# The hand-over from the recurrence to the expert layer: last logits laid out by a product, last row sums on VectorE, the end of the router moved into the first phase

## The reference, cut to what matters

```
xn = x * rsqrt(mean(x*x) + 1e-6) * norm_w ; x_branch, gate = split(xn @ W_in.T)
xc = silu(conv4(x_branch)) ; dt = clamp(softplus(xc @ W_dt.T + b)) ; B, C = xc @ W_B.T, xc @ W_C.T
h[t] = h[t-1] * exp(clamp(dt*A)) + dt*B*xc ; every 10th step h *= min(20/|h|, 1)
y = sum over n of h*C + D*xc            (16 states n per channel)
x2 = layernorm(x + (x + scale * (y*silu(gate)) @ W_out.T))
p = softmax(x2 @ w_router) ; the two largest of 8 experts per token, gates p/(p1+p2)
place of a token in its expert = running count over the 8192 tokens, kept if below 768
out = layernorm(x2 + sum of gate * expert(x2))      (expert: 256 -> 1024 -> relu -> 256)
```

## Time and profile before

| what | us |
|---|---|
| median of three executions | 2680.76 |
| the profiled execution, its own time | 2680.78 |
| its span in the trace | 2678.6 |
| last operation of the first phase (VectorE, LGS) | 2277.6 |
| first operation of the second phase | 2281.1 |
| first product of the counts | 2288.4 |

### The profile page before, as it was taken

The page is one execution under the profiler, slowest core; times in us unless marked ns, Lnnn a source line. Parts: engine busy times, 40 slices in busy tenths (PEclk is TensorE's granted clock), DMA queues, the critical chain, the costliest instruction groups (busy, mean ns, idle before and its releaser), DMA issues. The chain is left out here.

```text
span 2678.6 us, 50407 instructions
## 1 busy us (share of the span) xinstructions
PE 2564.4 (96%) x16600; PEld 2364.2 (88%) x16600; DVE 2376.2 (89%) x3459; ACT 2207.0 (82%) x4934; POOL 2189.3 (82%) x2270
## 2 busy tenths in 40 slices
PE   7999999999999999999999999999999988899997
PEld 6899999999999999999999999999999987677775
DVE  6999999999999999999999999999999998412245
ACT  5999999999999999999999999999999994211122
POOL 4898888889888888989888888989888896654546
PEclk9999999999999999999999999999999999699999
DMA  3222222222222222222222222222222222443464
GB/s 98 63 75 80 78 82 76 80 76 80 75 80 79 77 80 79 77 80 75 79 79 81 77 78 77 75 80 78 80 76 83 70 78 58 136 100 69 109 209 145
DMA packets 147569, 228.26 MB, mean 85 GB/s; under 512 B 39660, under 2 KB 85612, under 8 KB 146156
## 3 DMA queue, kind: packets, MB, share of 16 engines
q1 hardware_dynamic: 124228, 189.22, 24.2%
q0 software_dynamic: 11040, 15.15, 3.0%
q10 hardware_dynamic: 12040, 20.67, 2.3%
HBM read 190.85 MB, written 34.10 MB: 84 GB/s over the span
## 5 line engine op out<-in xcount | busy, mean ns | idle before, releaser
L1065 POOL TENSOR_TENSOR H<-H,CB 128x640 f32<-128x640 f32 (+1 forms) x824 | 1206.0, 1478 | 122.8 <-DVE H L808 120.9
L808 DVE TENSOR_TENSOR_SCAN H<-DA,PM 128x704 f32<-128x704 f32 (+1 forms) x824 | 1297.4, 1595 | 0.0
L521 ACT ACTIVATE DA<-DT,SM 128x160 f32<-128x160 f32 (+1 forms) x3200 | 1068.9, 422 | 1.5 <-POOL DT L956 0.3
L1101 PE MATMUL YB<-H,ID 128*128 128x160 f32 (+1 forms) x6592 | 1032.5, 308 | 0.2 <-POOL H L1065 0.2
L1101 PEld LDWEIGHTS YB<-H,ID 128*128 128x128 f32 x6592 | 971.2, 190 | 16.4 <-issue 11.2
L776 DVE TENSOR_TENSOR PM<-PM,BB 128x640 f32<-128x640 f32 (+1 forms) x824 | 667.4, 810 | 0.2
L530 ACT ACTIVATE DA<-DA 128x2560 f32<-128x2560 f32 x204 | 473.1, 2320 | 1.7
L973 POOL TENSOR_TENSOR FC<-SN,HALF 128x4 f32<-128x4 f32 x206 | 232.4, 1128 | 38.7 <-DVE SN L815 34.7
L1114 PE MATMUL PAZ<-XN,RB 128*128 128x160 f32 x1648 | 249.6, 305 | 7.8 <-POOL XN L940 4.4
L1124 PEld LDWEIGHTS PAZ<-XB,CD 128*128 128x128 f32 x1664 | 237.5, 188 | 16.8
L1124 PE MATMUL PAZ<-XB,CD 128*128 128x160 f32 x1664 | 243.1, 297 | 0.0
(11 more groups left out here) (205 smaller groups left out, 2968.0 us busy)
## 6 DMA issues: line engine op xcount, KB each, us to landing
BB<-Bd SPq DMA_DIRECT2D x208, 320.0 KB, 3.4
CB<-Cd SPq DMA_DIRECT2D x206, 320.0 KB, 3.4
W<-in_w ACTq DMA_DIRECT2D x16, 1024.0 KB, 8.1
XT<-in_xT SPq DMA_DIRECT2D x52, 160.0 KB, 2.2
XR<-in_xp SPq DMA_DIRECT2D x208, 40.0 KB
X2d<-VV SPq DMA_DIRECT2D x208, 40.0 KB
YA<-VV SPq DMA_DIRECT2D x208, 40.0 KB
XFB<-YA SPq DMA_DIRECT2D x6, 1024.0 KB, 11.9
```

The costliest lines, as they stand in the source:

```text
L521: eng.activation(DA[:, c0:c0 + k1, :, a, m, 1:11].rearrange("p c b t -> p b c t"), DT[:, j % 2, a].rearrange("p b (c t) -> p b c t", c=2)[ ...
L808: eng.tensor_tensor_scan(H[:, q % 3, u, 0:n], decays(c, g)[:, u], DBX(u)[:, 0:n], 0.0, ALU.mult, ALU.add).then_inc(s_scan, 1)
L1065: eng.tensor_tensor(h, h, cb, ALU.mult).then_inc(s_hc, 1)
L1101: mm = eng.matmul(yv, ID[:], hv[:, :, :, n, 0:w], start=False, stop=n == 15)
```

## The change

Late logits. A table SEL (80 x 260, a new input) holds two selection matrices and a mask. For blocks 50 and 51 VectorE spreads the logits over a column group per batch row, times the mask (`logits_by_batch`, in the place of the copy LGS), and TensorE multiplies by the selection matrices, adding both blocks in one bank (PM, columns 1536 to 1599). VectorE adds this to `late.lg`, into which SyncE has read the rows already known (94 of 128) over a tile of zeros. The late router follows in the first phase. LGd is no longer written for these two blocks.

Last quarter. The sixteen products for q = 207 go. VectorE sums over n with four `tensor_reduce`, adds D*xc, and multiplies by the gate (`last_sums`, `last_z`).

Order. In i = 52 the parts of the early router are placed anew, and the logits of block 50 are taken off before the rest of its choices, so that the bank is free for the transposes.

Beside that: GpSimd's negation of the mean (L1070) goes in all 52 blocks, and L883 now waits for `s_x2`. The first 514 columns of the tables are loaded by SyncE in i = 52, into the place of XT. In the second phase LAST is copied by GpSimd instead of VectorE, and the weights of the second expert are loaded after the counting.

```diff
--- before.py
+++ after.py
@@ sync_program, first phase
-                    if s == 1 and ok(i - 3) and i - 3 < NB - 1:
+                    if s == 1 and ok(i - 3) and i - 3 < NB - 2:
                         lg_out(eng, i - 3)
...
+                    if s == 3 and i == NB:
+                        eng.wait_ge(s_xn, NB)
+                        eng.dma_start(MCA, d["consts"][:, 0:514]).then_inc(s_mc, 16)
+                        eng.dma_start(SEL, d["sel"]).then_inc(s_mc, 16)
+                        lg_written(eng, NB - 3)
+                        known = T * (NB - 2) - 10 - 128 * EARLY
+                        eng.wait_ge(s_slot, 2)
+                        eng.dma_start(late.lg[0:known], LGd[0:known, 8 * EARLY:64]).then_inc(s_mc, 16)
@@ scalar_program
-            lg_out(eng, NB - 1)
-            lg_written(eng, NB - 1)
+            eng.wait_ge(s_er, 20)
+            eng.activation(late.p, late.p, ACT.Exp).then_inc(s_ee, 1)
@@ vector_program
+            def last_sums():
+                q, c = NQ - 1, NC - 1
+                k, w = cols(c), rows(c)
+                h = H[:, q % 3, :, 0:64 * k].rearrange("p u (a n t) -> p u a t n", a=4, n=16)
+                for u in range(4):
+                    eng.wait_ge(s_hc, states(q, u))
+                    eng.tensor_reduce(YL[:, u], h[:, u, :, 0:w], AX.X, ALU.add).then_inc(s_yl, 1)
+                eng.wait_ge(s_dx, NB)
+                eng.wait_ge(s_dxh, NB - 1)
+                eng.wait_ge(s_yl, 4)
+                eng.tensor_tensor(YL, YL, vw(DX[:, (NB - 1) % 2, :, 4:8, 10:10 + w]), ALU.add).then_inc(s_yl, 1)
...
+            def logits_by_batch(j):
+                eng.wait_ge(s_lg, j + 1)
+                eng.wait_ge(s_mc, 48)
+                eng.tensor_tensor(LB[:, j % 2], PA[0:80, 320:336].rearrange("p (g e) -> p g e", g=2).unsqueeze(2).to_broadcast(
+                    [80, 2, 4, 8]), SEL[:, 256:260].unsqueeze(1).unsqueeze(3).to_broadcast([80, 2, 4, 8]),
+                    ALU.mult).then_inc(s_lgs, 1)
...
-                            eng.wait_ge(s_sd, i - 1)
+                            eng.wait_ge(s_x2, 2 * (i - 1))
...
-                    if u == 0 and 2 <= q - 3 < NQ:
-                        z_out(q - 3)
-
-                    if s == 6 and i == NB:
+                    if s == 4 and i == NB:
+                        last_sums()
                         eng.wait_ge(s_el, 32)
                         eng.wait_ge(s_dtp, 2 * NB)
                         logits_less_top(eng, early, s_er, 0)
+                    if u == 0 and 2 <= q - 3 < NQ - 1:
+                        z_out(q - 3)
+                    if s == 4 and i == NB:
+                        last_z()
+
+                    if s == 6 and i == NB:
                         eng.wait_ge(s_ee, 1)
                         probabilities(eng, early, s_er, 2)
-                    if s == 9 and i == NB:
-                        choice(eng, early, 0, s_er, 5)
+                        choice_masked(eng, early, 0, s_er, 5)
                     if s == 14 and i == NB:
+                        logits_by_batch(NB - 2)
+                        choice_first(eng, early, 0, s_er, 5)
                         choice(eng, early, 1, s_er, 11)
-                        both_choices(eng, early, s_er, 16)
...
+            logits_by_batch(NB - 1)
+            both_choices(eng, early, s_er, 16)
+            eng.wait_ge(s_op, NB + 1)
+            eng.tensor_tensor(late.lg, late.lg, LATE, ALU.add).then_inc(s_er, 1)
+            eng.wait_ge(s_er, 18)
+            logits_less_top(eng, late, s_er, 18)
+            eng.wait_ge(s_ee, 2)
+            probabilities(eng, late, s_er, 20)
+            choice(eng, late, 0, s_er, 23)
+            choice(eng, late, 1, s_er, 29)
+            both_choices(eng, late, s_er, 34)
@@ gpsimd_program
-                        eng.tensor_scalar(NM[:], MVR[:, :, 0], -1.0, 0.0, ALU.mult, ALU.add).then_inc(s_ve, 1)
...
+                            eng.tensor_scalar(VV[:, g], VV[:, g], MVR[:, g, 0:1], SD[:, g:g + 1],
+                                              ALU.subtract, ALU.mult).then_inc(s_x2, 1)
+                    if s == 4 and i == NB:
+                        eng.wait_ge(s_gt, 2 * NB)
+                        eng.memset(late.lg, 0.0).then_inc(s_slot, 1)
@@ tensor_program
-                if not 2 <= q < NQ:
+                if not 2 <= q < NQ - 1:
...
+                    if s == 9 and i == NB + 1:
+                        eng.wait_ge(s_lgs, NB - 1)
+                        eng.matmul(PM[:, 1536:1600], SEL[:, 0:128], LB[:, 0].rearrange("p g b e -> p (g b e)"),
+                                   start=True, stop=False)
...
+            eng.wait_ge(s_lgs, NB)
+            eng.matmul(PM[:, 1536:1600], SEL[:, 128:256], LB[:, 1].rearrange("p g b e -> p (g b e)"),
+                       start=False, stop=True).then_inc(s_op, 1)
@@ moe_phase
-            eng.dma_start(late.lg, LGd[:, 8 * EARLY:64]).then_inc(s_lg, 16)
...
-            eng.dma_start(MC[:, 0:514], d["consts"][:, 0:514]).then_inc(s_ld, 16)
-            eng.dma_start(MC[:, 514:1378], d["consts"][:, 514:1378]).then_inc(s_ld2, 16)
+            eng.dma_start(MC[:], d["consts"][:, 514:1378]).then_inc(s_ld2, 16)
...
             load_w(0)
-            load_w(1)
...
+            load_w(1)
             eng.wait_ge(s_bl, 32)
...
-            eng.memset(LAST[:, :, 0:1], 0.0).then_inc(s_last, 1)
-            eng.tensor_copy(LAST[:].rearrange("p e (b j) -> p (e b) j", j=8)[:, :, 1:8],
-                            MM.rearrange("p e (b j) -> p (e b) j", j=8)[:, :, 0:7]).then_inc(s_last, 1)
-            eng.wait_ge(s_lg, 16)
-            logits_less_top(eng, late, s_rt, 1)
...
-            both_choices(eng, late, s_rt, 17)
             eng.tensor_tensor(LAST[:].rearrange("p e (b j) -> p b j e", j=8)[:, 1:8, 0], late.oh[0][:, 0:7], late.oh[1][:, 0:7],
                               ALU.add).then_inc(s_last, 1)
...
+            eng.tensor_copy(LAST[:].rearrange("p e (b j) -> p (e b) j", j=8)[:, :, 1:8],
+                            MM.rearrange("p e (b j) -> p (e b) j", j=8)[:, :, 0:7]).then_inc(s_zg, 1)
+            eng.memset(LAST[:, :, 0:1], 0.0).then_inc(s_zg, 1)
             eng.memset(GG[:], 0.0).then_inc(s_zg, 1)
...
                 eng.matmul(cum(t), MM[:, e].rearrange("p e j -> p (e j)"), UPTO, start=True, stop=False)
-                eng.wait_ge(s_last, 3)
+                eng.wait_ge(s_zg, 2)
+                eng.wait_ge(s_last, 1)
                 eng.matmul(cum(t), LAST[:, e].rearrange("p e j -> p (e j)"), PAST, start=False, stop=True).then_inc(s_cum, 1)
```

More of the change, by code:

```diff
@@ L189, in ssm_phase @@
         s_el, s_er, s_ee = sem("el"), sem("er"), sem("ee")
+        s_yl, s_mc = sem("yl"), sem("mc")
         s_zero, s_xch, s_bc0, s_lim0, s_log0 = sem("zero"), sem("xch"), sem("bc0"), sem("lim0"), sem("log0")
         s_arg, s_argp, s_da0, s_as = sem("arg"), sem("argp"), sem("da0"), sem("as")
-        early = Part(Router(RB, IOE), 0, EARLY)
+        early, late = Part(Router(RB, IOE), 0, EARLY), Part(Router(RB, IOE), EARLY, 8)
+        LATE = PM[:, 1536:1600].rearrange("p (b e) -> p b e", e=8)
         KD = 0.5 / (0.0495 + 1e-8)
@@ L830, in z_out, with last_z @@
                                   ALU.mult).then_inc(s_z, 1)
+            def last_sums():
[9 more added lines that the diff above has]
+                eng.tensor_tensor(YL, YL, vw(DX[:, (NB - 1) % 2, :, 4:8, 10:10 + w]), ALU.add).then_inc(s_yl, 1)
+            def last_z():
+                w = rows(NC - 1)
+                eng.wait_ge(s_yl, 5)
+                eng.tensor_tensor(vw(Z[:, :, 4:8, 10:10 + w]), YL, vw(SG[:, (NB - 1) % 2, :, 4:8, 10:10 + w]),
+                                  ALU.mult).then_inc(s_z, 1)
+            def logits_by_batch(j):
+                eng.wait_ge(s_lg, j + 1)
+                eng.wait_ge(s_mc, 48)
+                eng.tensor_tensor(LB[:, j % 2], PA[0:80, 320:336].rearrange("p (g e) -> p g e", g=2).unsqueeze(2).to_broadcast(
+                    [80, 2, 4, 8]), SEL[:, 256:260].unsqueeze(1).unsqueeze(3).to_broadcast([80, 2, 4, 8]),
+                    ALU.mult).then_inc(s_lgs, 1)
             conv_gate_half(1)
@@ L927, in vector_program @@
                         gate(i + 1)
-                    if s == 15 and ok(i - 2):
+                    if s == 15 and ok(i - 2) and i - 2 < NB - 2:
                         j = i - 2
@@ L1306, in _, with moe_phase @@
                 tensor_program(eng)
-def moe_phase(nc, d, YA, X2d, LGd, GD, out, RB, IO):
+def moe_phase(nc, d, YA, X2d, GD, out, RB, IO, MCA):
     ctx = ExitStack()
@@ L1326, in moe_phase @@
         XFB = sb("XFB", [128, 6, 8, 256])
-        MC = sb("MC", [128, 1378])
-        ID, UPTO, PAST, PRIOR = [MC[:, 128 * n:128 * n + 128] for n in range(4)]
-        STRIDE, SLOT, AT, HALFWAY = MC[:, 512:514], MC[:, 514:1282], MC[:, 1282:1330], MC[:, 1330:1378]
+        MC = sb("MC", [128, 864])
+        ID, UPTO, PAST, PRIOR = [MCA[:, 128 * n:128 * n + 128] for n in range(4)]
```

(15 more changed lines are left out.)

31 lines of the change are left out of this document (13 added, 18 removed).

## The result

The changed kernel takes 2717.82 us (median of four, 2717.33 to 2718.61) against 2680.77 us: a ratio of 1.014, with a 95% interval of 1.0127 to 1.0153. It is **37 us slower**, where 8.6 us less were forecast.

A forecast was written before the change was run, and what follows sets the result against it. VectorE was taken to bound the first phase, a serial chain the hand-over, TensorE the experts. The hand-over's 8.35 us plus 0.25 made 8.6 off 2680.78: 2672.2 us, range 2669.5 to 2676.5.

The forecast's parts named there:

- step 1: GpSimd without L1070: 0.27 us less per block, covered by VectorE in steady blocks; 0.25 us gained once before the end.
- The slower rival: First-phase blocks: L713 falls on GpSimd's L1065, 0.46 us each, 23.5 us over 51 blocks; 2695.7 us, chance 0.05.
- 3, residual sum: VectorE's residual sum, after the exponential's wait and six operations: at 2265.8 instead of 2268.52, 2.7 us earlier.
- 4, transposes of block 51: GpSimd's scaling, lasting 2.46 to 2.8 us, ends at 2270.2; transposes start there, was 2274.82; logits at 2272.8.
- Step 2: Sums over n on VectorE, four reductions 1.4 us, covered by its wait: output product starts 2261.5, ends 3.3 us earlier.
- step 5: VectorE's early choices, 5.2 us plus 0.75 for contention with GpSimd's scaling: `logits_by_batch`(51) begins at 2273.6.
- step 6: Late choices, selection product, sum and 4.65 us late router to 2279.6; second phase begins at 2279.95, was 2281.11.
- step 7: LAST copied on GpSimd, 0.7 us with memset: second product of a pair at 2280.85, 8.35 us earlier.
- the rival of the late tables: Second phase: SLOT or ScalarE's count copies become the new wait; SLOT 3.7 us late, 2675.9 us, chance 0.12.
- Step 8: Counts and L1860 stay at the low clock: no gain or loss, bounds 1.5 us to each side.
- the clock rival: Clock falls earlier, output product at half speed, or late rise at experts: some 2.4 us more, 2674.6 us, chance 0.12.

The follow-up runs named there:

- add_of_moments: Kernel before without the negation, the scaling adding the mean straight from the moments' column: 2699.02 us against 2700.56.
- sums_back: Changed kernel with negation and addition back, last quarter's sums on TensorE again: 30.60 us from quarter 206's sums to the 48 products, against 28.28; no total given.
- choices_first: Changed kernel with negation and addition back, block 50's logits taken off after the early choices: 31.31 us for quarter 206's sums to the 48 products, against 28.28.

## Why the prediction was wrong, point by point

**The step that failed is step 1.** It counted what the edit of GpSimd's scaling takes away (L1070, 0.27 us) and not what it puts in its place. Steps 1 and 4 let the scaling last as long with `ALU.subtract` as with `ALU.add`, without bounds, though no row of before shows a subtraction of this form. It takes 2.2 times as long: 1226 ns for 556, 1.34 us more a block for the two halves. Less the 0.27 us of L1070, GpSimd is 1.08 us later to its state products, and VectorE's dt times x is held for 0.82 us a block. The step's term for the blocks was nothing; measured are 41.2 us.

**The slower rival named the way and not the cause.** L713 falling on L1065 in each block is what happened, and the price of 0.46 us was for one collision of 960 ns; measured are 0.83 us a block and 41.2 us in all (it said 23.5). It got 0.05, and the argument against it, that L1065 moves away by 0.27 us, rested on the same unpriced operation. "GpSimd mostly waits for VectorE's scan and so falls back in step" was true of most of the block, and not of slot 3 to slot 6, where it has no wait and 0.2 us of slack: 0.08 between the end of its state products and VectorE's product (1042.12 and 1042.20) and 0.14 because a held product ends 0.36 us after them and a free one 0.50 after its own start. That was in the timeline of before and was not looked for.

**"VectorE covers it"** holds for GpSimd being earlier (the addition without the negation won nothing in the blocks), and not for its being later: a busy VectorE is not a VectorE that waits for nobody, since a hold counts as busy.

**The steps of the hand-over** can be read from the version with the negation back, on a like chip. It is not the kernel that was forecast, since L1070 is in it:

| step | predicted, us | measured, us |
|---|---|---|
| 2, output product starts | 2261.5 | 2262.14 |
| 3, residual sum | 2265.8 | 2266.26 |
| 4, transposes of block 51 | 2270.2 | 2270.99 |
| 5, `logits_by_batch`(51) | 2273.6 | 2273.64 |
| 7, second product of the counts | 2280.85 | 2280.67 |
| all | 2672.2 | 2670.62 |

Step 2's reductions are longer than sized (2.14 us for the four, not 1.4), so the last output product wins 2.7 us where 3.3 were taken. The choices are less held than in step 5: the eight operations last 5.34 us where 5.2 + 0.75 were taken. So VectorE in the end waits 0.27 us for the logits instead of being 0.8 us late. That step 5 comes out within 0.04 us is luck: the residual sum came 0.46 us later than taken and the choices ran 0.6 us shorter. Redone, the terms of step 6 add up to 2279.7 and not 2279.6, and step 7's 0.7 leads from 2279.95 to 2280.65; the 0.2 more has no row. In the changed kernel itself this part was spoiled by the subtraction too (31.29 against 28.01 us from the sums of quarter 206 to the 48 products).

**Step 7.** LAST on GpSimd was 0.56 us and 0.12, as taken; the second product started when the first ended (2280.65) and waited for neither. The 0.97 for this copy that was estimated from the Trainium skill (GPSIMD Engine Reference, Elementwise — side-by-side cycle accounting), whose 2.6 cycles an element are stated there for two inputs where a copy has one, does not agree with the 0.56. MC landed in 3.4 us and nothing waited for it; the rival of the late tables fell.

**Step 8.** In the changed kernel the clock rival came true in part, by a way it had not named: TensorE idled for the scaling, and the output product took 1.6 us more, of its 2.4. Behind the counting the version with the negation back wins 1.4 us more (383.7 from the start of the 48 products to the end, for 385.1): 1.1 of them because these products took 15.11 us for 16.25, with a granted clock of 0.81 in their first 3 us and 0.50 behind. That is within the bounds of step 8, but it isn't shown to come from the change: in add_of_moments, whose hand-over is that of before, they took 15.11 us too, and in the runs sums_back and choices_first 16.24 and 16.23. So some 8.5 of the 10.0 us are the hand-over's (36.53 to 28.01), and 1.1 may be luck.

**The rule on the shared port.** The prediction weighed it in step 5 and for L713. The Trainium skill (SBUF — State Buffer, Who interferes with whom) says that a VectorE operation with two SBUF inputs and a GpSimd operation that reads SBUF exclude each other for a whole instruction. The traces agree: dt times x, both of whose inputs are in SBUF, is held for the whole rest of a state product and ends 0.36 us after it, while L798 (one input in PSUM) stays at 810 ns beside the same products (814 before).

## What to carry to other kernels

An operation that replaces another is to be priced by itself, even if only its opcode changes; where the trace has no row for it, the bounds are as wide as for any new operation, and in a loop they are multiplied by its count. An engine with idle time may still have no slack at one place of the loop: look how far apart the two engines' operations are there, in the timeline, before calling a change covered. And "busy all the time" includes being held: a mean duration that differs between two kernels for the same shape is the first thing to compare.

## What the runs showed of the hardware that was not expected

- On GpSimd a `tensor_scalar` of 80 x 256 f32 with a column operand takes 1226 to 1229 ns with subtract and multiply, 552 to 556 ns with add and multiply, whichever of the two tiles the operand is in. The reason is open.
- GpSimd's small memsets follow each other closely: five of 128 x 16 in 0.29 us. A power of 80 x 2 takes 0.69.
- VectorE's product of two SBUF tiles behind GpSimd's product of 128 x 640: 0.50 us free, up to 1.6 us when it comes into a state product, and it ends 0.36 us after that.
